# A Mamba tower on one core: convolution at unit 14, tokens at units 26 to 29, two early decays, rstd in PSUM, a hinted loop

## Chip, cores and metric

One core of one Trainium2 chip. The time is that of one execution on the device in microseconds (us); lower is better.

## What is computed

32 images of 256 x 256 x 4 become 257 tokens of 256 channels each. Layer 0 runs four Mamba blocks on every image, two forward and two backward, and merges them; a mixture of experts follows, then attention and a feed-forward part that keeps half of the tokens. The change touches the Mamba blocks alone:

```python
def _mamba_block(x, in_w, conv_w, conv_b, A_log, xd_w, xB_w, xC_w, dtp_w, dtp_b, D, out_w, g, b):
    xn = _layer_norm(x, g, b)
    xs, z = jnp.split(xn @ in_w, 2, axis=-1)
    xc = silu(causal depthwise conv of xs, 4 taps, + conv_b)
    delta = jax.nn.softplus(xc @ xd_w @ dtp_w + dtp_b)
    Bm, Cm = xc @ xB_w, xc @ xC_w
    dA = jnp.exp(delta[..., None] * -jnp.exp(A_log))
    dBx = (delta * xc)[..., None] * Bm[:, :, None, :]
    y = _ssm_scan(dA, dBx, Cm) + D * xc          # h = dA * h + dBx; y = sum_n h * C
    return y * jax.nn.silu(z) @ out_w + x
```

512 inner channels (4 groups of 128) with 16 states each; all in float32.

## The kernel before

`mamba_phase` writes out the queue of every engine by hand. The images go in 16 groups of two; a group has four **jobs**, one for each block (0, 2, 1, 3 in this order). A job has 64 scans, one for each of 4 channel groups and 16 states, over both images at once (128 partitions x 512 tokens). Two scans make a **unit**: 32 units a job. Job 0 of the first group and the last three jobs are unrolled; in between a loop of 15 iterations runs jobs 1, 2, 3 and 4, where job 4 is the first job of the next group (`run`). Each engine has its own loop, without a barrier.

For state s the work goes through the engines like this:

- ScalarE: `decays` writes exp(delta x a) to one of `NDP` = 2 PSUM banks (`decay`), two states ahead of the scan.
- GpSimd: `b_times_u` writes b x u to one of four buffers (`bu`); for every fourth state, s % 4 == 1 (`POOL_C`), it also multiplies h by c.
- VectorE: `scan`, and `c_times_h` for the other three of four states. So an even unit has two scans and one product, an odd one two and two.
- TensorE: `add_state` transposes ch into `y_ps` and adds it up (4 transposes a state). After 16 states ScalarE copies the sum (`token_rows`), TensorE turns it back (`channel_rows`), and VectorE multiplies it by the gate (`output`): y0 to y2 within the job, y3 in unit 1 of the next.

Beside the scans of job jj the engines prepare job jj + 1, at the units that the functions `after_even` and `after_odd` of ScalarE and the `period`s of TensorE and VectorE name: the gates and their Silu (units 5 to 9), centring and variance (from `norm_at`), the inverse deviation as exp(-0.5 ln(var + eps)), the input product, the convolution from `CONV_AT` = 15, its Silu at unit 24, projections (`xp`), the four step inputs (`dt0` to `dt3`) and the softplus of the step size. A Silu needs another table in ScalarE than Exp and Ln do, so two table loads stand around it. In job 2 the tokens of the next group are built as well (`tokens`, 64 matmuls on TensorE in four quarters, then two copies on ScalarE), from eight pieces of x that SP brings into two buffers (`load_x`).

All these products go to three PSUM banks, `w_ps`, which are handed round by a list of keys (`preparation`, `one_job`, `later_keys`): key i may write its first bank when key i - 2 has been read, and its second when key i - 1 has:

```python
def banks(name, g, jj):
    odd = slot(name, g, jj) % 2
    if bank_count(name) == 1:
        return w_ps[:, 2 * odd, :]
    return w_ps[:, 2:0:-1, :] if odd else w_ps[:, 0:2, :]
```

When the projections are there, SP stores b and c and reads them back, broadcast to all partitions, in eight pairs of 514 KB transfers (`bring_bc`). The rest of the program, `tail_phase`, is the same before and after.

## Time and profile before

| | |
|---|---|
| median of 3 runs | 10373.58 us (10369.56 to 10376.43) |
| profiled execution | 10389.18 us; its span 10387.4 us |
| busy: TensorE, VectorE, ScalarE, GpSimd | 8344 us (80%), 8088 (78%), 5899 (57%), 7060 (68%) |
| mean granted clock of TensorE | 0.87 |
| the Mamba stage (144 to 8662 us) | 8518 us, 64 jobs |

The profile names an instruction by its line, engine, operation and the tiles it writes and reads; PE is TensorE, PEld its weight loads, DVE VectorE, ACT ScalarE, POOL GpSimd. A "wait" is idle time of an engine and what ended it. A granted clock of 1.00 is 2.4 GHz, 0.50 is 1.2 GHz. An fp32 matmul shows as two instructions, a transpose as one. The shares of the whole span mix the Mamba stage with the tail, so they say little of either.

### The profile page before, as it was taken

What the parts mean: (1) busy time and instruction counts of PE and PEld (TensorE: products, weight loads), DVE (VectorE), ACT (ScalarE), POOL (GpSimd) and SP (SyncE); (2) the same over time, 40 slices, a digit from 0 to 9 for tenths busy, and PEclk for the clock granted to TensorE, in tenths of its full rate; (3) what the DMA queues carried; (4) which work ended last, traced back from release to release, by engine and by line L of the source; (5) the groups of instructions that cost most, each with busy time, mean ns of one, the idle gap of its engine ahead of it and who ended that gap; (6) DMA issues with size and microseconds to landing.
All of it is one profiled execution on the core that took longest, in us unless ns stands there. A gap on an engine that the chain in (4) does not pass through costs nothing. (4 is left out here: it accounts for less than half of the span.)

```text
span 10387.4 us, 152898 instructions
## 1 busy us (share of the span) xinstructions
PE 8344.1 (80%) x42776; PEld 6881.5 (66%) x42776; DVE 8087.7 (78%) x10482; ACT 5899.2 (57%) x9202; POOL 7059.5 (68%) x7227
## 2 busy tenths in 40 slices
PE   5877777777878787878787877787877776999998
PEld 4666666666666666666666666676666664777776
DVE  4888889888988888888898888888888894333332
...
GB/s 93 94 89 99 92 98 91 99 92 93 92 94 93 90 98 93 90 79 90 89 98 93 98 91 97 93 98 92 90 93 96 92 90 25 11 10 10 12 9 9
DMA packets 414916, 819.68 MB, mean 79 GB/s; under 512 B 148919, under 2 KB 194139, under 8 KB 414043
## 3 DMA queue, kind: packets, MB, share of 16 engines
...
## 5 line engine op out<-in xcount | busy, mean ns | idle before, releaser
L776 ACT ACTIVATE decay<-delta,neg_a 128x512 f32<-128x512 f32 x4096 | 2793.0, 688 | 2484.5 <-DVE h_ps L978 1112.7
L544 POOL TENSOR_TENSOR bu<-b_all,u_buf 128x512 f32<-128x512 f32 x3072 | 3579.4, 1191 | 151.6 <-DVE h_ps L978 148.3
L978 DVE TENSOR_TENSOR_SCAN h_ps<-decay,bu 128x512 f32<-128x512 f32 x2304 | 2782.6, 1222 | 454.6 <-ACT decay L776 376.3
L1233 PE MATMUL y_ps<-ident,ch 128*128 128x128 f32 x16384 | 2579.9, 309 | 637.4 <-DVE ch L998 362.7
L1233 PEld LDWEIGHTS y_ps<-ident,ch 128*128 128x128 f32 x16384 | 2226.7, 161 | 1016.2 <-DVE ch L998 484.4
L556 POOL TENSOR_TENSOR ch<-ch,c_all 128x512 f32<-128x512 f32 x1024 | 1325.5, 1294 | 1112.1 <-DVE ch L978 910.0
L998 DVE TENSOR_TENSOR ch<-h_ps,c_all 128x512 f32<-128x512 f32 x3072 | 1977.2, 671 | 0.0
L547 POOL TENSOR_TENSOR bu<-b_all,u_buf 128x514 f32<-128x514 f32 x1024 | 1245.6, 1237 | 66.8 <-issue 56.3
L1117 PE MATMUL w_ps<-xn,in_w 128*128 128x257 f32 x4096 | 1074.8, 408 | 170.5 <-ACT xn L665 83.6
L982 DVE TENSOR_TENSOR_SCAN h_ps<-decay,bu 128x256 f32<-128x256 f32 x1536 | 1046.7, 737 | 125.3 <-POOL bu L547 98.2
L1117 PEld LDWEIGHTS w_ps<-xn,in_w 128*128 128x128 f32 x4096 | 799.9, 206 | 320.2 <-issue 81.1
L1576 POOL TENSOR_TENSOR rstd_F<-h_F 128x514 f32<-128x514 f32 x16 | 17.5, 1095 | 1429.1 <-DMA h_F<-h_mid 1429.1
L978 DVE TENSOR_TENSOR_SCAN ch<-decay,bu 128x512 f32<-128x512 f32 x768 | 926.2, 1206 | 55.4 <-ACT decay L776 54.0
L1117 PE MATMUL w_ps<-xs_pad,diag_store 128*128 128x257 f32 x4096 | 950.9, 380 | 0.0
L1117 PEld LDWEIGHTS w_ps<-xs_pad,diag_store 128*128 128x128 f32 x4096 | 746.5, 190 | 91.3
L1117 PE MATMUL w_ps<-dtbc,dt_w 32*128 32x257 f32 x1024 | 443.4, 551 | 247.9 <-ACT dtbc L707 127.6
L1117 PE MATMUL w_ps<-sz,out_w 128*128 128x257 f32 x2048 | 507.4, 391 | 119.1 <-ACT x_b L762 59.1
L1117 PEld LDWEIGHTS w_ps<-sz,out_w 128*128 128x128 f32 x2048 | 379.6, 193 | 182.8 <-ACT x_b L762 66.5
L1226 PE MATMUL y_ps<-skip_diag,xc 128*128 128x128 f32 x2048 | 347.4, 324 | 172.6 <-ACT y_t L751 172.5
L1117 PEld LDWEIGHTS w_ps<-dtbc,dt_w 32*128 32x128 f32 x1024 | 216.2, 246 | 391.6 <-ACT rstd L718 184.7
L1226 PEld LDWEIGHTS y_ps<-skip_diag,xc 128*128 128x128 f32 x2048 | 317.1, 232 | 215.8 <-ACT y_t L751 211.0
L1245 PE MATMUL w_ps<-ident,y_t 128*128 128x128 f32 x1024 | 187.5, 314 | 259.1 <-ACT y_t L751 259.1
(258 smaller groups left out, 11583.9 us busy)
## 6 DMA issues: line engine op xcount, KB each, us to landing
b_all<-bc_dram SPq DMA_DIRECT2D x512, 514.0 KB, 8.6
c_all<-bc_dram SPq DMA_DIRECT2D x512, 514.0 KB, 10.0
...
diag_store<-diag_dram SPq DMA_DIRECT2D x256, 256.0 KB, 2.9
x_in<-in_x SPq DMA_DIRECT2D x128, 256.0 KB, 2.6
...
skip_diag<-skip_dram SPq DMA_DIRECT2D x64, 256.0 KB, 4.1
...
```

The lines of the kernel that those rows point to most:

```text
L544: pool.tensor_tensor(bu[:, s % NBU, 0:NB * L].rearrange("p (b t) -> p b t", b=NB), b_all[:, n // NU, n % NU, :, 1:], u_buf[:, c % 2, :, 1: ...
L547: pool.tensor_tensor(bu[:, s % NBU, :], b_all[:, n // NU, n % NU, :, :].rearrange("p b s -> p (b s)"), u_buf[:, c % 2, :, :].rearrange("p ...
L556: pool.tensor_tensor(h, h, c_all[:, n // NU, n % NU, :, 1:], ALU.mult).then_inc(pool_c_done, 1)
L776: func(decay[:, s % NDP, :].rearrange("p (b t) -> p b t", b=NB), delta[:, c, :, 1:S], ACT.Exp, scale=neg_a[:, k, c, n:n + 1]).then_inc(dec ...
L978: dve.tensor_tensor_scan(h, decay[:, s % NDP, :], bu[:, s % NBU, 0:NB * L], 0.0, ALU.mult, ALU.add).then_inc(scan_done, 1)
L982: last = dve.tensor_tensor_scan(h[:, cols], decay[:, s % NDP, cols], bu[:, s % NBU, b * S + 1:(b + 1) * S], bu[:, s % NBU, b * S:b * S + 1 ...
L998: dve.tensor_tensor(ch[:, s % NPR, :].rearrange("p (b t) -> p b t", b=NB), h_ps[:, h_slot(s), :].rearrange("p (b t) -> p b t", b=NB), c_al ...
L1117: last = pe.matmul(w[0:rows, b, 0:S], lhs, rhs, start=(i == 0), stop=(i == len(terms(b)) - 1))
L1226: pe.matmul(y_ps[:, k, :], xc[:, jj % 2, c, b, 1 + half * P:1 + (half + 1) * P], skip_diag[:, jj % 2, c, :], start=(k == 0), stop=False, s ...
L1233: last = pe.matmul(y_ps[:, k, :], ch[:, s % NPR, k * P:(k + 1) * P], ident[:, :], is_transpose=True, start=False, stop=(n == NST - 1 and k ...
L1245: last = pe.matmul(w[:, k * P:(k + 1) * P], y_t[:, k, :], ident[:, :], is_transpose=True, start=True, stop=True, skip_group_check=True)
L1576: pool.tensor_tensor(rstd[s][:, :, :], h[s][:, 0, :, :], h[s][:, 1, :, :], ALU.add).then_inc(h_summed[s], 1)
```

## The change

- The convolution starts at unit 14, and all that follows it comes a unit earlier: the Silu at unit 23, projections at 24, step inputs at 25, 26, 30 and 31. y2 is turned at unit 26 instead of 25; y1 stays at 18, where the convolution's second half used to begin behind it and now comes ahead.
- Decays 50 and 51 (`EARLY`) go to two banks of `w_ps` that idle between the convolution and the projections, right ahead of the Silu (`early_decays`). The copy of the rows of y2 comes behind the Silu.
- The tokens' products move from units 10 to 13 of job 2 to units 26 to 29, their two copies on ScalarE to 28 and 30. SP asks for the first two pieces of x at the start of job 2 and for the others between the pairs of `bring_bc`.
- The inverse deviation stays in its PSUM banks; the products with it stand inside unit 13, and the gain and bias half a unit earlier. After a job 4 the normalization starts at unit 10, not 11.
- The loop carries a hint for the branch back.

```diff
@@ -25,7 +25,8 @@
...
 BLOCK_OF_JOB = (0, 2, 1, 3)
-CONV_AT = 15
+CONV_AT = 14
+EARLY = 2 * (CONV_AT + 9) + 4, 2 * (CONV_AT + 9) + 5
 EPS = 1e-5
@@ -49,8 +50,7 @@
...
-        first = norm[:2] + ["t0"] + norm[2:] + ["t1"] if tokens else norm
-        steps = first + conv + ["xp", "dt0", "dt1", "dt2", "dt3"]
+        steps = norm + conv + ["early", "xp", "dt0", "dt1"] + (["t0", "t1"] if tokens else []) + ["dt2", "dt3"]
         return [(name, 4 if name in ("t0", "t1") else jj) for name in steps]
@@ -66,10 +66,8 @@
...
-        for name, before in [("y2", "xp"), ("y1", "cv1")] + [("y0", "t1"), ("y0", "xs0")]:
+        for name, before in [("y2", "dt1"), ("y1", "xs2"), ("y0", "xs0")]:
             at = [i for i, key in enumerate(keys) if key[0] == before]
-            if name == "y0" and ((name, jj) in keys or before == "t1" and not at):
-                continue
             keys = keys[:at[0]] + [(name, jj)] + keys[at[0]:] if at else [(name, jj)] + keys
@@ -102,14 +100,14 @@
...
     def y_at(jj):
-        return (14 if jj == 4 else 12), CONV_AT + 3, CONV_AT + 10
+        return (14 if jj == 4 else 12), 18, 26
...
     def norm_at(jj):
-        return 11 if jj == 4 else 9
+        return 10 if jj == 4 else 9
@@ -246,7 +244,7 @@
...
         rstd_ready = sem("rstd_ready")
-        xhat_ready = sem("xhat_ready")
+        rstd_logs = sem("rstd_logs")
         xn_ready = sem("xn_ready")
@@ -314,7 +312,7 @@
...
             period(0, 0, True, False)
-            with eng.Fori(0, GROUPS - 1) as g:
+            with nc.Fori(0, GROUPS - 1, engines=[eng.engine], hint_back_edge=True) as g:
                 for jj in (1, 2, 3, 4):
@@ -388,10 +386,12 @@
...
-            def load_x(g, jj):
-                for n in range(8):
+                    if jj == 3 and not is_final(g) and n in (1, 2, 3):
+                        load_x(g, 4, (2 * n, 2 * n + 1))
+            def load_x(g, jj, part=range(8)):
+                for n in part:
                     c, b, half = n // 4, n // 2 % 2, n % 2
@@ -433,6 +433,8 @@
...
+                if jj == 2 and not is_final(g):
+                    load_x(g, 4, range(2))
                 if not first:
@@ -443,8 +445,6 @@
...
                     load_weights(jj + 1)
-                    if jj == 2 and not is_final(g):
-                        load_x(g, 4)
                     load_skip(g, jj + 1)
@@ -653,6 +653,12 @@
...
                 w = banks(name, g, jj)
+                if kind == "job":
+                    func(w[:, :, 0:S], w[:, :, 0:S], ACT.Ln, bias=eps_t[:, 0:1]).then_inc(rstd_logs, 1)
+                    act.wait_ge(rstd_logs, job_count(g, jj, 1, 1))
+                    func(w[:, :, 0:S], w[:, :, 0:S], ACT.Exp, scale=-0.5).then_inc(rstd_ready, 1)
+                    return
                 func(rstd[:, :, :], w[:, :, 0:S], ACT.Ln, bias=eps_t[:, 0:1]).then_inc(read_of(name, g, jj), 1)
@@ -660,7 +666,7 @@
...
                 k = BLOCK_OF_JOB[jj % 4]
-                act.wait_ge(xhat_ready, job_count(g, jj, 1, 1))
+                act.wait_ge(read_of("var", g, jj), nth("var", g, jj))
                 for c in range(CM):
@@ -761,7 +767,19 @@
...
-            def decays(g, jj, s):
+            def early_decays(g, jj):
+                k = BLOCK_OF_JOB[jj % 4]
+                w = banks("early", g, jj + 1)
+                for c in (2, 3):
+                    act.wait_ge(read_of(f"cv{c}", g, jj + 1), nth(f"cv{c}", g, jj + 1))
+                for i, s in enumerate(EARLY):
+                    c, n = s // NST, s % NST
+                    func(w[:, i, :].rearrange("p (b t) -> p b t", b=NB), delta[:, c, :, 1:S], ACT.Exp,
+                         scale=neg_a[:, k, c, n:n + 1]).then_inc(decays_ready, 1)
+                act.sem_inc(full_of("early", g, jj + 1), 1)
+            def decays(g, jj, s, behind=0):
@@ -771,8 +789,8 @@
...
-                if positive(job_count(g, jj, STATES, s + 1 - NDP)):
-                    act.wait_ge(scan_done, job_count(g, jj, STATES, s + 1 - NDP))
+                if positive(job_count(g, jj, STATES, s + 1 - NDP - behind)):
+                    act.wait_ge(scan_done, job_count(g, jj, STATES, s + 1 - NDP - behind))
                 func(decay[:, s % NDP, :].rearrange("p (b t) -> p b t", b=NB), delta[:, c, :, 1:S], ACT.Exp,
@@ -817,6 +835,9 @@
...
                     conv_output(g, jj, c + 1)
+                act.wait_ge(read_of("cv3", g, jj), nth("cv3", g, jj))
+                act.sem_inc(full_of("early", g, jj), 1)
+                act.sem_inc(read_of("early", g, jj), 1)
                 conv_silu(g, jj)
@@ -846,11 +867,11 @@
...
                     centred(g, jj + 1, 1)
-                if jj == 2 and not is_final(g) and u == 12:
-                    tokens(g, 4, 0)
+                if jj == 2 and not is_final(g) and u in (28, 30):
+                    tokens(g, 4, (u - 28) // 2)
                 if u == norm_at(jj) + 3:
                     inverse_deviation("job", g, jj + 1)
-                if u == norm_at(jj) + (4 if jj == 4 else 5):
+                if jj == 4 and u == norm_at(jj) + 4:
                     gain_and_bias(g, jj + 1)
@@ -885,8 +906,8 @@
...
                     centred(g, jj + 1, 0)
-                if jj == 2 and not is_final(g) and u == 14:
-                    tokens(g, 4, 1)
+                if jj != 4 and u == norm_at(jj) + 4:
+                    gain_and_bias(g, jj + 1)
                 if u == CONV_AT + 1:
@@ -902,18 +923,21 @@
...
+                if not last and s in EARLY:
+                    return
                 if not (last and s >= STATES):
-                    decays(g, jj, s)
+                    decays(g, jj, s, behind=NDP if not last and s - NDP in EARLY else 0)
...
                     lead(g, jj, NU * u + NDP, last)
-                    if u % PAIRS == 1 and u // PAIRS != 3 and not (first and u == 1):
+                    if u % PAIRS == 1 and not (first and u == 1):
                         token_rows(g, jj - (u == 1), (u // PAIRS - 1) % CI)
...
                     lead(g, jj, NU * u + NDP + 1, last)
-                    if u == silu_at(jj)[1]:
-                        token_rows(g, jj, u // PAIRS - 1)
+                    if NU * u + 2 * NDP in EARLY and not last:
+                        early_decays(g, jj)
                     after_odd(g, jj, u, first, last)
@@ -940,9 +964,10 @@
...
                 dst = x_f if kind == "tok" else cen
+                inverse = rstd[:, :, :] if kind == "tok" else banks("var", g, jj)[:, :, 0:S]
                 for c in range(CM):
-                    last = dve.tensor_tensor(dst[:, c, :, :], cen[:, c, :, :], rstd[:, :, :], ALU.mult)
-                last.then_inc(x0_ready if kind == "tok" else xhat_ready, 1)
+                    last = dve.tensor_tensor(dst[:, c, :, :], cen[:, c, :, :], inverse, ALU.mult)
+                last.then_inc(x0_ready if kind == "tok" else read_of("var", g, jj), 1)
@@ -961,7 +986,18 @@
...
-            def scan(g, jj, s, b):
+            def decay_of(g, jj, s, last):
+                if s in EARLY and not last:
+                    return banks("early", g, jj + 1)[:, EARLY.index(s), :]
+                return decay[:, s % NDP, :]
+            def early_read(g, jj):
+                dve.wait_ge(scan_done, job_count(g, jj, STATES, EARLY[-1] + 1))
+                dve.sem_inc(read_of("early", g, jj + 1), 1)
+            def scan(g, jj, s, b, last):
                 inside = s not in POOL_C
@@ -975,7 +1011,7 @@
...
-                    dve.tensor_tensor_scan(h, decay[:, s % NDP, :], bu[:, s % NBU, 0:NB * L], 0.0, ALU.mult, ALU.add
+                    dve.tensor_tensor_scan(h, decay_of(g, jj, s, last), bu[:, s % NBU, 0:NB * L], 0.0, ALU.mult, ALU.add
                                            ).then_inc(scan_done, 1)
@@ -1053,23 +1089,27 @@
...
                     for b in range(NB if s < NST else 1):
-                        scan(g, jj, s, b)
+                        scan(g, jj, s, b, last)
                     if u - 1 in y_at(jj):
                         output(g, jj, y_at(jj).index(u - 1))
+                    if jj != 4 and not last and u == norm_at(jj) + 4:
+                        normalize("job", g, jj + 1)
                     if jj == 4 and u in (6, 8):
...
                         step_size(*size, 0)
-                    scan(g, jj, s + 1, 0)
+                    scan(g, jj, s + 1, 0, last)
                     if s + 1 in POOL_C and s < NST:
                         c_times_h(g, jj, s)
-                        scan(g, jj, s + 1, 1)
+                        scan(g, jj, s + 1, 1, last)
                     else:
                         if s < NST:
-                            scan(g, jj, s + 1, 1)
+                            scan(g, jj, s + 1, 1, last)
                         c_times_h(g, jj, s)
...
                             c_times_h(g, jj, s + 1)
+                    if s in EARLY and not last:
+                        early_read(g, jj)
                     if size:
@@ -1084,7 +1124,7 @@
...
                         normalize("tok", g, 4)
-                    if u == norm_at(jj) + (3 if jj == 4 else 4):
+                    if jj == 4 and u == norm_at(jj) + 3:
                         normalize("job", g, jj + 1)
@@ -1298,8 +1338,6 @@
...
                         centre(g, jj + 1, [u - norm_at(jj)])
-                    if jj == 2 and not is_final(g) and 10 <= u < 14:
-                        tokens(g, 4, (u - 10) // 2, (u - 10) % 2)
                     if u == norm_at(jj) + 2:
@@ -1321,6 +1359,8 @@
...
                         step_input(g, jj + 1, steps.index(u))
+                    if jj == 2 and not is_final(g) and 26 <= u < 30:
+                        tokens(g, 4, (u - 26) // 2, (u - 26) % 2)
```

**Place 1**, ScalarE around the Silu of the convolution in job 1. L692 (now L698) copies the convolution's last output, L751 (L757) the rows of y2, L698 and L699 (L704, L705) load the tables. Before:

```order
L692 ACTIVATE xc<-w_ps,conv_b 128x514
L775 REGISTER_ALU
L776 ACTIVATE decay<-delta,neg_a 128x512
L751 ACTIVATE y_t<-y_ps 128x512
L698 ACT_TABLE_LOAD
L698 ACTIVATE xc<-xc 128x2056
L699 ACT_TABLE_LOAD
L775 REGISTER_ALU
L776 ACTIVATE decay<-delta,neg_a 128x512
L775 REGISTER_ALU
L776 ACTIVATE decay<-delta,neg_a 128x512
```

Now:

```order
L698 ACTIVATE xc<-w_ps,conv_b 128x514
L793 REGISTER_ALU
L794 ACTIVATE decay<-delta,neg_a 128x512
L778 ACTIVATE w_ps<-delta,neg_a 128x512 x2
L704 ACT_TABLE_LOAD
L704 ACTIVATE xc<-xc 128x2056
L705 ACT_TABLE_LOAD
L793 REGISTER_ALU
L794 ACTIVATE decay<-delta,neg_a 128x512
L757 ACTIVATE y_t<-y_ps 128x512
L793 REGISTER_ALU
L794 ACTIVATE decay<-delta,neg_a 128x512
```

The two decays to `w_ps` are new ahead of the first table load, the copy of y_t has gone behind the second.

**Place 2**, TensorE behind the same Silu, in job 2. `xc,xp_w` are the projections, `dtbc,dt_w` a step input, `ident,y_t` turns y2, `skip_diag` starts the sum of the last 16 states. Before:

```order
L1221 REGISTER_ALU
L1226 MATMUL y_ps<-skip_diag,xc 128x128 x4
L1231 REGISTER_ALU
L1233 MATMUL y_ps<-ident,ch 128x128 x4
L1229 REGISTER_ALU
L1233 MATMUL y_ps<-ident,ch 128x128 x4
L1245 MATMUL w_ps<-ident,y_t 128x128 x4
L1117 MATMUL w_ps<-xc,xp_w 64x257 x8
L1231 REGISTER_ALU
L1233 MATMUL y_ps<-ident,ch 128x128 x4
L1231 REGISTER_ALU
L1233 MATMUL y_ps<-ident,ch 128x128 x4
```

Now:

```order
L1266 MATMUL y_ps<-skip_diag,xc 128x128 x4
L1271 REGISTER_ALU
L1273 MATMUL y_ps<-ident,ch 128x128 x4
L1269 REGISTER_ALU
L1273 MATMUL y_ps<-ident,ch 128x128 x4
L1153 REGISTER_ALU
L1157 MATMUL w_ps<-dtbc,dt_w 128x257 x2
L1271 REGISTER_ALU
L1273 MATMUL y_ps<-ident,ch 128x128 x4
L1271 REGISTER_ALU
L1273 MATMUL y_ps<-ident,ch 128x128 x4
L1285 MATMUL w_ps<-ident,y_t 128x128 x4
```

y2 stood ahead of the projections and now stands behind them, four states and the first step input.

**Place 3**, TensorE and the tokens (`tok_ident,x_in`, a quarter each) in job 2. Before, at units 12 and 13:

```order
L1139 ISA
L1165 REGISTER_ALU
L1117 MATMUL w_ps<-sq,mean_w 128x257 x4
L1231 REGISTER_ALU
L1233 MATMUL y_ps<-ident,ch 128x128 x4
L1231 REGISTER_ALU
L1233 MATMUL y_ps<-ident,ch 128x128 x4
L1245 MATMUL w_ps<-ident,y_t 128x128 x4
L1129 REGISTER_ALU
L1103 REGISTER_ALU
L1134 MATMUL w_ps<-tok_ident,x_in 128x128 x8
L1231 REGISTER_ALU
```

Now, at units 26 to 28:

```order
L1285 MATMUL w_ps<-ident,y_t 128x128 x4
L1157 MATMUL w_ps<-dtbc,dt_w 128x257 x2
L1169 ISA
L1143 REGISTER_ALU
L1174 MATMUL w_ps<-tok_ident,x_in 128x128 x8
L1271 REGISTER_ALU
L1273 MATMUL y_ps<-ident,ch 128x128 x4
L1269 REGISTER_ALU
L1273 MATMUL y_ps<-ident,ch 128x128 x4
L1169 REGISTER_ALU
L1174 MATMUL w_ps<-tok_ident,x_in 128x128 x8
L1179 ISA
```

The quarters stood between y0 and the variance and now follow the second step input.

## Rows read from the trace of the kernel before

**Rows 1.** Windows: start:end, us; busy of PE, PEld, DVE, ACT, POOL; clock, DMA, GB/s.
```profile
144.00:8662.00 8518.00, 6705.30 (x35260) 5612.55 (x35260) 7555.48 (x9297) 5135.84 (x7970) 7011.83 (x7164) 0.86 0.26 92
2537.00:2673.60 136.60, 113.99 (x594) 97.60 (x593) 116.81 (x146) 80.37 (x126) 109.35 (x113) 0.87 0.29 99
2945.10:3072.80 127.70, 98.95 (x530) 81.93 (x531) 116.32 (x145) 79.03 (x123) 108.33 (x112) 0.86 0.24 81
```

**Rows 2.** Waits of VectorE: us in total, times, longest.
```profile
DVE h_ps L978 <- ACT decay L776: 376.3, 251, 3.4
...
DVE diag_store L953 <- ACT sp_l L730: 75.7, 64, 39.2
```

**Rows 3.** Timeline, VectorE, a job 3 from unit 23: start, us, instruction, idle before.
```profile
2766.51 1.22 DVE L978 TENSOR_TENSOR_SCAN h_ps<-decay,bu 128x512 f32<-128x512 f32 x1
...
2767.98 1.23 DVE L978 TENSOR_TENSOR_SCAN h_ps<-decay,bu 128x512 f32<-128x512 f32 x1 [0.24 <-POOL bu L544]
...
2780.74 1.23 DVE L978 TENSOR_TENSOR_SCAN h_ps<-decay,bu 128x512 f32<-128x512 f32 x1 [3.35 <-ACT decay L776]
...
2784.61 2.33 DVE L978 TENSOR_TENSOR_SCAN h_ps<-decay,bu 128x512 f32<-128x512 f32 x2
...
2788.04 1.22 DVE L978 TENSOR_TENSOR_SCAN h_ps<-decay,bu 128x512 f32<-128x512 f32 x1
```

**Rows 4.** Timeline, ScalarE, the same stretch.
```profile
2775.40 1.28 ACT L698 ACT_TABLE_LOAD   x1
...
2776.70 1.93 ACT L698 ACTIVATE xc<-xc 128x2056 f32<-128x2056 f32 x1
...
2779.93 1.30 ACT L776 ACTIVATE decay<-delta,neg_a 128x512 f32<-128x512 f32 x2
```

**Rows 5.** Timeline, TensorE, the same stretch.
```profile
2776.43 1.04 PE L1233 MATMUL y_ps<-ident,ch 128*128 128x128 f32 x8
...
2777.30 0.60 PE L1245 MATMUL w_ps<-ident,y_t 128*128 128x128 f32 x4
...
2778.67 3.68 PE L1117 MATMUL w_ps<-xc,xp_w 128*64 128x257 f32 x16 [0.77 <-ACT xc L698]
...
2785.40 1.13 PE L1117 MATMUL w_ps<-dtbc,dt_w 32*128 32x257 f32 x4 [2.02 <-ACT dtbc L707]
...
2788.91 1.22 PE L1117 MATMUL w_ps<-dtbc,dt_w 32*128 32x257 f32 x2 [0.73 <-ACT rstd L718]
```

**Rows 6.** A window of the same job; the 0.50 is the granted clock.
```profile
2788.60:2795.30 6.70, 6.26 (x25) 5.21 (x26) 6.70 (x8) 6.20 (x11) 6.29 (x7) 0.50 0.99 301
```

**Rows 7.** Timeline: y1 in a job 3, its TensorE, and y1 in a job 2.
```profile
2753.66 0.69 DVE L1018 TENSOR_TENSOR sz<-w_ps,sz 128x512 f32<-128x512 f32 x1 [0.84 <-PE w_ps L1245]
...
2753.46 3.63 PE L1117 MATMUL w_ps<-xs_pad,diag_store 128*128 128x257 f32 x16
...
3158.16 0.69 DVE L1018 TENSOR_TENSOR sz<-w_ps,sz 128x512 f32<-128x512 f32 x1 [1.57 <-PE w_ps L1245]
```

**Rows 8.** Groups of VectorE: busy us, mean ns, idle before.
```profile
L944 DVE TENSOR_TENSOR cen<-cen,rstd 128x514 f32<-128x514 f32 x128 | 119.9, 975 | 36.4 <-ACT rstd L659 36.4
...
L933 DVE TENSOR_TENSOR cen<-h_next,w_ps 128x514 f32<-128x514 f32 x32 | 20.6, 688 | 56.9 <-PE w_ps L1117 56.9
```

**Rows 9.** Timeline: y0 in a job 2, and a quarter of the tokens.
```profile
3134.17 0.69 DVE L1018 TENSOR_TENSOR sz<-w_ps,sz 128x512 f32<-128x512 f32 x1 [7.65 <-PE w_ps L1245]
...
3126.30 4.08 PE L1134 MATMUL w_ps<-tok_ident,x_in 128*128 128x128 f32 x16
```

**Rows 10.** DMA issues: count, KB each, median us to landing.
```profile
c_all<-bc_dram SPq DMA_DIRECT2D x512, 514.0 KB, 10.0
...
x_in<-in_x SPq DMA_DIRECT2D x128, 256.0 KB, 2.6
```

**Rows 11.** Timeline: the back edge, VectorE and GpSimd.
```profile
2945.07 1.40 DVE L982 TENSOR_TENSOR_SCAN h_ps<-decay,bu 128x256 f32<-128x256 f32 x2 [5.03 <-POOL bu L547]
...
2942.41 1.27 POOL L547 TENSOR_TENSOR bu<-b_all,u_buf 128x514 f32<-128x514 f32 x1 [4.17 <-issue]
```

## Prediction

> **What bounds the kernel now.** I read the windows first. Over the stage that the change touches, which I cut out as one window of 8518 us, VectorE is busy 7555 us (89%), GpSimd 82%, TensorE 79% and ScalarE 60% [rows 1]. VectorE's order is fixed by hand, so the stage lasts as long as its work plus its waits; the other engines matter where it waits for them. A job (one block of one pair of images) is 32 units of two states: the window of a job 1 is 127.7 us with 116.3 us of VectorE work, that of a job 2 is 136.6 us with nearly the same work [rows 1]. Then the table of waits says whose fault the rest is: 376 us for decays from ScalarE and 76 us for the logarithm of the step size are the two of this stage that I need [rows 2]. The timelines of single jobs tell where in a job they lie. The reader should see there that the same waits come at the same unit of every job.
>
> **Part 1: the convolution a unit earlier, two decays ahead, y2 a unit later.** Between the starts of units 23 and 28 VectorE takes 2788.04 - 2766.51 = 21.5 us, 3.35 of them one wait for decay 52 [rows 3], since ScalarE loads a table (1.28), runs the Silu (1.93) and loads the old table back, as long again [rows 4] while only two decays lie ready. In the change the same work follows decay 49 and the two decays of the idle banks. Counted from the start of unit 23: state 47's scan is done at 2.6 (it starts at 1.47 [rows 3] and takes 1.2); decay 49 and two early ones at 0.65 each (two took 1.30 [rows 4]) end at 4.6; table and Silu end at 7.85, the second table and decay 52 at 9.8. VectorE without this wait reaches unit 26 at 2780.74 - 2766.51 - 3.35 = 10.9, so the stall goes entirely.
>
> What is late next is y2. After the Silu TensorE has the projections (3.6), the skip products (1.0, as many as the transposes of two states), two states (0.9), the first step input (1.1), two more states (0.9) and the transposes (0.6), by the rows of each [rows 5]: 7.85 + 8.1 = 15.9. VectorE is ready for y2 at 10.9 + 2.85 + 1.14 = 14.9 (the odd unit 27 takes 3.43, its two scans 1.14 each [rows 3]; an even one has a product less, 0.59). It waits 1.0, and after y2 (0.7, and 0.4 until the next scan starts), a scan and two products it is at unit 28 at 19.2, 2.3 us sooner than now.
>
> TensorE's clock comes on top. Now a convolution runs right up to the Silu; in the change it ends two units sooner, and some 6 us with 16 short transposes lie ahead of the projections. After such stretches the granted clock was 0.50 (1.2 GHz) in this kernel: in the window at 2788.6 two products of a step input took 1.22 us, where four had taken 1.13 before it [rows 5, 6]. Work on the path then costs up to double; a stretch of 6.7 us at half clock costs 3.4 us at most. I take 1.3 us a job (most jobs pay nothing or 1.7; not all fall into it), with bounds of 0 and 3.4. Net 1.0 us, times 63 jobs with a next job: **-63 us**. By the Trainium skill (TensorE: Matmul & The Clock Gate, Part 1) an array that has idled runs at 1.2 GHz and comes back to 2.4 only once it has been kept busy; it would put every job's projections at the half clock, and the sum by it is rival 2. The row of 0.50 agrees that such stretches occur; whether this one becomes one no run here shows.
>
> **Part 2: y1.** The unit of y1 stays 18, but the 16 products of convolution 1 now stand ahead of it. From the start of unit 17: copy of the rows at 2.5 (scan 1.2, decay 0.7, copy 0.6), skip 1.0, two states 0.9, convolution 3.5 [rows 7], two states 0.9, transposes 0.6: 9.4. VectorE wants it at 3.4 + 2.85 + 1.14 = 7.4, so it waits 2.0 instead of 0.84 [rows 7]. A job 2 waits 1.57 there already [rows 7], and I take jobs 4 to be like it, so I charge the 1.1 us to the 31 jobs 1 and 3: **+34 us** (bounds 0 and 63 x 1.5 = 95).
>
> **Part 3: the logarithm.** Everything behind the Silu comes a unit earlier, so the 0.58 us before the step size goes ((75.7 - 39.2) / 63 [rows 2]; the 39.2 is the first job's): **-36 us**. It could not give more, and costs nothing while TensorE is less than a unit late.
>
> **Part 4: inverse deviation in PSUM.** Two products a job now read rstd from PSUM. Read from SBUF they took 0.98 us each, and the same shape with a PSUM input 0.69 [rows 8]: 2 x 0.29 x 63 = **-37 us**. For the job after a job 4 the chain now starts in the very unit of the gate's Silu; I cost that at nothing: ScalarE's two centring copies come behind its Silu and eat what the earlier start brings.
>
> **Part 5: the tokens.** Now they sit at units 10 to 13 of job 2 and hold y0 back by 7.65 us [rows 9]. A job 2 is 8.9 us longer than a job 1 [rows 1]; less the 0.7 of y1, 8.2 us can go per group. In units 26 to 29 they hang on ScalarE instead: its copy of t0 stands ahead of decay 59. From the end of y2's transposes: step input 0.9, a quarter of the tokens 3.8 [rows 9], two states 0.9, the next quarter 3.8, and 1.3 for pieces of x that are asked for only when one is used up (2.6 us to land [rows 10]): 10.8. ScalarE then needs 2.7 for copy, powers and decay; VectorE comes for decay 59 at 7.4. So it waits 6.1 us, and 2.1 are left: 15 x 2.1 = **-31 us**, with bounds of -123 (no wait at all) and the loss of rival 3.
>
> **Part 6: the loop's back edge.** VectorE stands still for 5.03 us between the last instruction of job 4 and the first of job 1, waiting for GpSimd, whose own 4.17 us are put down to nothing but issue [rows 11]. Each engine's sequencer branches there for itself, so all of them stand still together. Nothing in this trace has a hinted branch; the bounds are 0 and all of it, 14 x 5.0. I take all of it, as GpSimd begins to stand still at 2942.41 - 4.17 = 2938.2 and VectorE only at 2945.07 - 5.03 = 2940.0 [rows 11]: without the branch GpSimd would have its first product of job 1 (1.27) ready in time: **-70 us**. The Trainium skill (Runtime: NRT & Kernel Launch, Instruction fetch mechanics) says that a taken branch to code not in the instruction memory waits for a DMA, and Advanced Engine Details and Errata (Control Flow Timing) gives some 108 ns for a compare-and-branch; by these the estimate would be 14 x 4.9 = 69 us.
>
> **Sum.** -63 + 34 - 36 - 37 - 31 - 70 = -203 us on a span of 10387.4. The profiled execution took 10389.2, 15.6 more than the median of the runs; from the median 10373.6 the sum gives 10170. What 0.2% (21 us) can't tell from no change, I count as the same.
>
> **Rivals.**
> 1. *The hint does nothing.* The stall at the first unit of job 1 stays at 5 us: 10240. Against it speaks only that the wait is pure issue. 0.12.
> 2. *TensorE is at half clock behind every Silu.* y2 waits 1.0 + 3.4 us: 63 x (3.4 - 1.3) = 132 more, 10302. For it: the granted clock falls wherever the work is thin [rows 6]. 0.13.
> 3. *The tokens starve ScalarE, and the kernel gets slower.* Between pieces of x SP now issues the 514 KB broadcasts of b and c, of which the latter takes 10.0 us to land where a piece takes 2.6 [rows 10]. If a piece queues behind them and lands after 10.0, each of the three turns costs 7.4: 6.1 + 22.2 = 28.3 us of waiting against 8.2 removed. That is +302 in the place of -31: 10373.6 - 172 + 302 = 10504. It decides from a landing of 7.6 us on (15 x (6.1 + 3 x 5.0 - 8.2) = 194 us). Against it: the broadcasts of a job come one pair per unit, and three pieces are asked for by then. 0.07.
> 4. *TensorE stays at full clock.* 63 x 1.3 = 82 less: 10088. 0.17.
> The forecast itself, within some 50 us of 10170, has 0.48, and 0.03 is left for mishaps of no one name.
>
> **How the numbers follow.** The likeliest case gives 10170. The range reaches down past case 4 with some of the tokens' bound (10050) and up to case 1 with half of case 2 (10290); rival 3 and the rest lie outside. Faster takes all but rival 3 and some of the rest: 0.88; same 0.04; slower 0.08.
>
> **What would show it.** The wait for a decay at unit 26 gone; a wait of 1 to 3 us at y2 in unit 27 (long with a granted clock of 0.50 there, short without); y1's wait at 2 us; the product with rstd at 0.69; unit 13 of job 2 as short as in job 1, and a wait of 6 us for decay 59 in it; the first scan of job 1 straight behind job 4. The prediction is wrong if GpSimd, with 82% now, becomes what VectorE waits for, if the tokens' wait is over 20 us, or if the projections start later than the Silu's end.

## The result, and the profile after

| | before | after |
|---|---|---|
| median of 4 runs each | 10375.01 us (10369.56 to 10381.79) | 10297.75 us (10291.67 to 10303.34) |
| ratio | | 0.9925, 95% interval 0.9908 to 0.9942 |
| profiled execution | 10389.18 us | 10301.12 us, span 10299.2 |
| end of the Mamba stage | 8662 us | 8569 us |

So the change is 77 us faster, where 203 were forecast, and the time lies just above the range (10290). The direction was right, and the size was not. (The two profiled executions differ by 88 us and their stages by 93, since the one before was 14 us above its median and the one after only 3.)

The windows of the changed kernel: the stage from 144 us to its end, then a job 1 and a job 2.

```profile
144.00:8569.30 8425.30, 6705.40 (x35260) 5524.77 (x35260) 7525.31 (x9298) 5134.66 (x7970) 6977.26 (x7164) 0.87 0.27 93
2906.97:3034.01 127.04, 99.98 (x530) 81.56 (x529) 116.44 (x146) 79.34 (x124) 108.92 (x113) 0.86 0.27 92
3034.01:3170.19 136.18, 111.80 (x589) 94.34 (x588) 115.88 (x145) 78.76 (x124) 109.53 (x113) 0.89 0.30 99
```

Against [rows 1] VectorE's work fell by 30 us and the stage by 93. A job 1 and a job 2 take what they took before, to 0.7 us. To see where the time went I cut every job of the loop at the first scan of some units, and took the difference of each stretch, mean of 15 iterations (us, after less before):

| units | 0-9 | 9-12 | 12-16 | 16-20 | 20-22 | 22-28 | 28-32 | job |
|---|---|---|---|---|---|---|---|---|
| job 1 | -0.1 | 0.0 | -1.7 | +1.3 | -0.3 | 0.0 | 0.0 | -0.8 |
| job 2 | 0.0 | 0.0 | -7.9 | -0.2 | -0.3 | +0.6 | +7.9 | +0.1 |
| job 3 | -0.5 | 0.0 | -0.8 | +1.1 | -0.3 | -1.1 | +0.1 | -1.5 |
| job 4 | -0.6 | -0.1 | -0.3 | +1.4 | -0.3 | +0.1 | -4.5 | -4.3 |
| all four | -1.2 | -0.1 | -10.7 | +3.6 | -1.1 | -0.4 | +3.5 | -6.5 |

-6.5 us by 15 iterations are -97. One column stands out by what it does not show: units 22 to 28, where the Silu is, give next to nothing (-0.4 for all four jobs). The tokens' 7.9 only change their place. The 4.5 at the end of job 4 are the back edge of the loop. Now the rows.

VectorE's waits in the stage. The wait for decays has grown from [rows 2], and that for the turned rows (`sz`) is large:

```profile
DVE h_ps L1014 <- ACT decay L794: 402.8, 178, 7.7
DVE sz L1054 <- PE w_ps L1285: 293.8, 214, 2.3
```

VectorE behind the Silu in a job 1, units 26 and 27 (start, duration, instruction, idle before it):

```profile
3007.26 1.20 DVE L1014 TENSOR_TENSOR_SCAN ch<-decay,bu 128x512 f32<-128x512 f32 x1
3008.37 0.67 DVE L1034 TENSOR_TENSOR ch<-h_ps,c_all 128x512 f32<-128x512 f32 x1
3010.68 1.23 DVE L1014 TENSOR_TENSOR_SCAN h_ps<-decay,bu 128x512 f32<-128x512 f32 x1 [1.64 <-ACT decay L794]
3013.79 0.69 DVE L1054 TENSOR_TENSOR sz<-w_ps,sz 128x512 f32<-128x512 f32 x1 [1.88 <-PE w_ps L1285]
3014.86 1.23 DVE L1014 TENSOR_TENSOR_SCAN h_ps<-decay,bu 128x512 f32<-128x512 f32 x1 [0.38 <-POOL bu L544]
```

The stall of 3.35 at unit 26 [rows 3] is gone, and three waits stand a unit later, 3.9 us together. ScalarE and TensorE of the same stretch, both cut to the chain:

```profile
3002.04 1.92 ACT L704 ACTIVATE xc<-xc 128x2056 f32<-128x2056 f32 x1
3003.97 1.28 ACT L705 ACT_TABLE_LOAD   x1
...
3009.39 0.59 ACT L713 ACTIVATE dtbc<-w_ps 64x514 f32<-64x514 f32 x1 [2.33 <-PE w_ps L1157]
3009.88 1.29 ACT L794 ACTIVATE decay<-delta,neg_a 128x512 f32<-128x512 f32 x2
```

```profile
3004.01 5.26 PE L1157 MATMUL w_ps<-xc,xp_w 128*64 128x257 f32 x16 [3.34 <-ACT xc L704]
3009.20 1.16 PE L1266 MATMUL y_ps<-skip_diag,xc 128*128 128x128 f32 x8
3010.20 1.04 PE L1273 MATMUL y_ps<-ident,ch 128*128 128x128 f32 x8
3011.16 1.13 PE L1157 MATMUL w_ps<-dtbc,dt_w 32*128 32x257 f32 x4
3012.22 1.09 PE L1273 MATMUL y_ps<-ident,ch 128*128 128x128 f32 x8
3013.15 0.60 PE L1285 MATMUL w_ps<-ident,y_t 128*128 128x128 f32 x4
```

TensorE stands idle 3.34 us for the Silu, then takes 5.26 us for the projections. ScalarE's copy of them (L713) stands in its queue ahead of decay 54, so VectorE waits for decay 54 until 3010.6. The turn of y2 comes behind 3.9 us of other work. The windows of the idle time, the first half of the projections and the time behind it (the third number from the end is the granted clock):

```profile
3001.00:3004.00 3.00, 0.00 (x0) 0.00 (x0) 3.00 (x5) 2.97 (x3) 3.00 (x3) 0.97 0.00 0
3004.00:3007.20 3.20, 3.19 (x8) 1.80 (x9) 3.20 (x4) 3.04 (x4) 3.20 (x4) 0.50 0.00 0
3007.30:3010.00 2.70, 2.70 (x16) 1.76 (x15) 1.74 (x3) 0.61 (x2) 2.31 (x7) 1.00 0.00 0
```

The group of all projections, the changed kernel and then, in a fence of its own, the kernel before (busy us, mean ns of one, idle time ahead):

```profile
L1157 PE MATMUL w_ps<-xc,xp_w 128*64 128x257 f32 x1008 | 343.1, 515 | 212.8 <-ACT xc L704 212.8
```

```profile
L1117 PE MATMUL w_ps<-xc,xp_w 128*64 128x257 f32 x1008 | 232.0, 382 | 48.4 <-ACT xc L698 48.4
```

Job by job it is plainer still: before, TensorE idled 0.77 us ahead of the projections and they took 3.68 us in 63 of 64 jobs; after, it idles 3.3 to 3.4 us and they take over 4 us in 55 of 64 jobs (median 5.36, up to 6.62). The 60 jobs of the changed kernel's loop sort themselves by it (us, mean in brackets):

| projections took | jobs | VectorE's wait for decay 54 | its wait for y2 | units 22 to 28 |
|---|---|---|---|---|
| 3.68 | 9, all of them jobs 3 | none | 1.69 | 22.3 to 22.4 |
| 5.22 to 5.37 | 33 | 1.25 to 1.75 (1.54) | 1.88 | 23.9 to 24.4 (24.25) |
| 6.40 to 6.61 | 18, 12 of them jobs 2 | 2.43 to 2.72 (2.55) | 1.88 | 25.1 to 25.5 (25.20) |

Before, units 22 to 28 took 24.35 us in every job. So a job at full clock gains 2.0 us there, most jobs gain 0.1, and the longest projections lose 0.85. The whole difference passes through the wait for decay 54; the wait for y2 hardly moves. In the nine jobs of the first row TensorE had stood idle just as long (3.3 us) as in the others.

The groups of VectorE that changed (rstd read from PSUM, to be held against [rows 8]; the step size's first instruction), and the back edge, where VectorE's first scan of job 1 now starts without a wait (L983 is the last work of job 4):

```profile
L978 DVE SCALAR_TENSOR_TENSOR diag_store<-diag_store 128x514 f32<-128x514 f32 x127 | 121.7, 958 | 0.0
...
L969 DVE TENSOR_TENSOR cen<-cen,w_ps 128x514 f32<-128x514 f32 x126 | 81.2, 687 | 13.9 <-DVE sz L1054 10.8 <-ACT w_ps L660 3.0
```

```profile
2906.17 0.88 DVE L983 SCALAR_TENSOR_TENSOR cen<-cen,sq 128x514 f32<-128x514 f32 x1
2906.97 1.39 DVE L1018 TENSOR_TENSOR_SCAN h_ps<-decay,bu 128x256 f32<-128x256 f32 x2
```

The tokens in a job 2: VectorE in unit 29, ScalarE's copy with the decay behind it, and TensorE's quarters:

```profile
3156.71 1.23 DVE L1014 TENSOR_TENSOR_SCAN h_ps<-decay,bu 128x512 f32<-128x512 f32 x1 [6.97 <-ACT decay L794]
```

```profile
3154.05 0.69 ACT L623 ACTIVATE h_next<-w_ps,tok_wb 128x512 f32<-128x512 f32 x1 [6.41 <-PEq L1180]
...
3155.92 0.67 ACT L794 ACTIVATE decay<-delta,neg_a 128x512 f32<-128x512 f32 x1
```

```profile
3143.27 4.00 PE L1174 MATMUL w_ps<-tok_ident,x_in 128*128 128x128 f32 x16
...
3149.82 4.10 PE L1174 MATMUL w_ps<-tok_ident,x_in 128*128 128x128 f32 x16 [1.67 <-DMA x_in<-in_x]
```

### The profile page after: what moved, and what is told of

The parts are those of the page before. It is cut to its first block and busy times, and to the rows that moved or that the text cites. A ratio compares the mean times of both kernels' runs of the same rounds, so it can differ in the third digit from the quotient of the medians.

```text
span 10299.2 us, 152957 instructions
## 1 busy us (share of the span) xinstructions
PE 8347.5 (81%) x42776; PEld 6796.5 (66%) x42776; DVE 8057.0 (78%) x10482; ACT 5898.0 (57%) x9202; POOL 7025.0 (68%) x7227
## 5 line engine op out<-in xcount | busy, mean ns | idle before, releaser
L794 ACT ACTIVATE decay<-delta,neg_a 128x512 f32<-128x512 f32 x3970 | 2712.6, 688 | 2269.8 <-DVE h_ps L1014 1062.9
L1014 DVE TENSOR_TENSOR_SCAN h_ps<-decay,bu 128x512 f32<-128x512 f32 x2178 | 2629.7, 1222 | 503.9 <-ACT decay L794 402.8
L1273 PE MATMUL y_ps<-ident,ch 128*128 128x128 f32 x16384 | 2488.7, 300 | 552.9 <-DVE ch L1034 434.6
L1273 PEld LDWEIGHTS y_ps<-ident,ch 128*128 128x128 f32 x16384 | 2111.7, 155 | 926.9 <-DVE ch L1034 578.5
L1157 PE MATMUL w_ps<-xn,in_w 128*128 128x257 f32 x4096 | 1104.4, 415 | 157.8 <-ACT xn L671 63.9
L1157 PE MATMUL w_ps<-xc,xp_w 128*64 128x257 f32 x1024 | 348.5, 515 | 217.0 <-ACT xc L704 217.0
L1157 PE MATMUL w_ps<-dtbc,dt_w 32*128 32x257 f32 x1024 | 398.2, 510 | 77.8 <-ACT rstd L724 75.3
L1157 PEld LDWEIGHTS w_ps<-xc,xp_w 128*64 128x64 f32 x1024 | 185.0, 187 | 366.6 <-issue 213.0
```

The costliest lines, as they stand in the source:

```text
L794: func(decay[:, s % NDP, :].rearrange("p (b t) -> p b t", b=NB), delta[:, c, :, 1:S], ACT.Exp, scale=neg_a[:, k, c, n:n + 1]).then_inc(dec ...
L1014: dve.tensor_tensor_scan(h, decay_of(g, jj, s, last), bu[:, s % NBU, 0:NB * L], 0.0, ALU.mult, ALU.add).then_inc(scan_done, 1)
L1157: last = pe.matmul(w[0:rows, b, 0:S], lhs, rhs, start=(i == 0), stop=(i == len(terms(b)) - 1))
L1273: last = pe.matmul(y_ps[:, k, :], ch[:, s % NPR, k * P:(k + 1) * P], ident[:, :], is_transpose=True, start=False, stop=(n == NST - 1 and k ...
```

## The experiments

Each was timed beside the kernel before, in five rounds. The groups of runs had their own kernel before (medians 10384, 10375 and 10383 us), so the times are compared by their ratios; a ratio is known to about 0.0013, 14 us, and the difference of two gains a little worse than that. "Gain" below is one less the ratio, times 10375, in us; the changed kernel has 78 by that.

| run | median us | ratio, 95% interval | gain |
|---|---|---|---|
| e1_hint_alone | 10301.42 | 0.9923, 0.9909 to 0.9936 | 80 |
| e2_hint_and_rstd | 10322.97 | 0.9947, 0.9934 to 0.9961 | 55 |
| e9_norm_at_10 | 10316.78 | 0.9934, 0.9920 to 0.9948 | 68 |
| e3_tokens_at_10 | 10351.10 | 0.9971, 0.9959 to 0.9983 | 30 |
| the change | 10297.75 | 0.9925, 0.9908 to 0.9942 | 78 |
| e10_rstd_in_sbuf | 10331.40 | 0.9950, 0.9937 to 0.9964 | 52 |
| e4_y2_first | 10209.98 | 0.9832, 0.9819 to 0.9846 | 174 |
| e5_warm | 10209.86 | 0.9838, 0.9824 to 0.9851 | 168 |
| e6_y1_first | 10230.99 | 0.9859, 0.9844 to 0.9874 | 146 |
| e11_y1_and_copy | 10243.43 | 0.9868, 0.9853 to 0.9883 | 137 |
| e7_both_and_softplus | 10216.38 | 0.9844, 0.9830 to 0.9857 | 162 |
| e8_both_and_warm | 10104.35 | 0.9740, 0.9726 to 0.9753 | 270 |
| e12_all_and_copy | 10051.02 | 0.9679, 0.9666 to 0.9692 | 333 |

**From the kernel before to the change, one part at a time.** First the hint alone, on the kernel before.

```diff
-            with eng.Fori(0, GROUPS - 1) as g:
+            with nc.Fori(0, GROUPS - 1, engines=[eng.engine], hint_back_edge=True) as g:
```

> The kernel before with the hinted loop and nothing else. My theory: the 5.0 us that VectorE stands still at the first unit of job 1 go, 14 to 15 times, and nothing else moves: 70 to 75 us less, about 10302. That would be nearly all that the whole change gave (77 us), so the other five parts together would give nothing. Rival: the stall only went because the changed order around it left GpSimd ahead; then the hint alone gives under 35 us and the first wait of job 1 stays above 2 us.

It gave 80, all that the whole change gives. The forecast of part 6 was 70; the waits inside the jobs stay nearly as they were (1.5 us less over four jobs). So the other parts come to nothing together.

Added to it, the inverse deviation in PSUM, its two uses at their old places.

```diff
+                if kind == "job":
+                    func(w[:, :, 0:S], w[:, :, 0:S], ACT.Ln, bias=eps_t[:, 0:1]).then_inc(rstd_logs, 1)
+                    act.wait_ge(rstd_logs, job_count(g, jj, 1, 1))
+                    func(w[:, :, 0:S], w[:, :, 0:S], ACT.Exp, scale=-0.5).then_inc(rstd_ready, 1)
+                    return
...
+                inverse = rstd[:, :, :] if kind == "tok" else banks("var", g, jj)[:, :, 0:S]
```

> The kernel before with the hint and the inverse deviation left in PSUM, its products with it at their old place. My theory: two products a job at 0.69 us in the place of 0.98 give 37 us more than the hint, about 10265, which is faster than the changed kernel. Rival: GpSimd, whose share is 82%, or the bank that is now held until VectorE has read it (for y0 and the first input product) gives it back: within 10 us of the hint alone.

25 us slower than e1, not 37 faster. The first theory fell, and the rival was right in its second half: jobs 1, 3 and 4 got shorter by 0.5, 1.3 and 1.6 us, but a job 2 longer by 4.7, in a new wait of 4.85 us for a decay at unit 16. TensorE there:

```profile
3102.86 0.60 PE L1252 MATMUL w_ps<-ident,y_t 128*128 128x128 f32 x4
3108.33 4.00 PE L1141 MATMUL w_ps<-tok_ident,x_in 128*128 128x128 f32 x16 [4.86 <-DVE cen L951]
```

The second half of the tokens may write its first bank only when the variance's banks have been read. That used to be done by ScalarE's logarithm; now it is done by VectorE's product, which stands behind the late y0. And ScalarE's copy of those tokens stands ahead of a decay. A part that is worth 37 us by its own instruction costs 25 where another part is missing.

Next the convolution with everything that hangs on it. The changed kernel with only the tokens put back differs from e2 in just that (convolution and Silu a unit earlier, early decays, y1 and y2, and the normalization of job 4).

```diff
-                    if jj == 2 and not is_final(g) and 26 <= u < 30:
-                        tokens(g, 4, (u - 26) // 2, (u - 26) % 2)
...
+                    if jj == 2 and not is_final(g) and 10 <= u < 14:
+                        tokens(g, 4, (u - 10) // 2, (u - 10) % 2)
```

> The changed kernel with the tokens' products, their copies, their keys and SP's loads of x back at units 10 to 14 of job 2. My theory: in the changed kernel the tokens cost 8.7 us of waiting for decays at units 29 and 31 of job 2 and about 0.7 at unit 27, in the old place 7.7 before y0: so the same within 1 us a group, 10283 to 10313. Rival, my prediction's part 5: the old place is 2.1 us a group dearer, 31 us more, 10329.

Parts 1, 2 and 3 and job 4 together: from e2 (55) to e3 (30), 25 us lost, where the forecast had 63 + 36 - 34 = 65 gained. And the tokens' move, from e3 (30) to the change (78), gains 48, more than the 31 of part 5 and against my theory of 0: beside PSUM rstd the old place has e2's wait too. The two parts go together. (By the job table the move is worth nothing, -7.9 and +7.9 us; no run has it beside an rstd in SBUF against the same kernel without it.)

From e2 to e3 a job 4 went from 132.7 to 135.7 us (medians). Is it the normalization at unit 10? This run is e2 with that alone:

```diff
     def norm_at(jj):
-        return 11 if jj == 4 else 9
+        return 10 if jj == 4 else 9
```

> e2_hint_and_rstd (10323) with one number changed: the normalization after a job 4 starts at unit 10 in the place of 11, as in the changed kernel; the convolution stays at 15. It asks why a job 4 takes 135.7 us in the changed kernel and 132.7 in e2. Theory 1: the earlier centring, whose two copies on ScalarE now stand right behind the gate's Silu and ahead of decays 27 and 29, costs it: job 4 at 135 to 136, 15 x 3 = 45 more, about 10365. Theory 2: the convolution at 14 costs it: job 4 stays at 132.7 and the time is the same within 10 us.

A job 4 takes 133.0 us: theory 2. Its waits for decays at unit 13 do double (2.3 to 4.6 us), but of the 1.9 us that it waited at unit 14 for rstd and a decay 0.9 are left (now at unit 13), and y1's wait falls from 2.0 to 0.8: together they pay for it. With the convolution at 14 as well (e3) y1 waits 2.3 again, and 1.4 us for decays at units 17 and 18 come on top.

The other side of the pair: the changed kernel with part 4 taken back.

```diff
-                inverse = rstd[:, :, :] if kind == "tok" else banks("var", g, jj)[:, :, 0:S]
+                inverse = rstd[:, :, :]
```

> The changed kernel with the inverse deviation back in SBUF. In e2 against e1 PSUM cost 22 us, though each of the two products got 0.29 us shorter, since a job 2 got 4.4 us longer: its second half of the tokens stood behind the banks of the variance, and the copy of it ahead of a decay. Theory: in the changed kernel the tokens stand elsewhere, so PSUM gives what the products say, and without it the time is 37 us higher, 10325 to 10340. Rival: the products' gain is eaten by GpSimd or by the held banks here too, and it is the same within 10 us.

26 us by the ratios, 34 by the medians: theory, within the noise. Part 4 is worth most of its 37 where the tokens are out of its way. Not all of the difference is its own, though: without it the projections ran over 4 us in 63 of 64 jobs in the place of 55, and 0.8 of the 2.7 us by which the four jobs got longer lie in units 22 to 28.

**What stands behind the Silu.** Seven products ahead of the projections, in the idle time, into the bank that they will overwrite:

```diff
+            def warm(g, jj):
+                w = banks("xp", g, jj)
+                bank_free("xp", g, jj, 0)
+                for i in range(7):
+                    pe.matmul(w[0:RNK + 2 * NST, 0, 0:S], xp_w[:, i % CI, :], xc[:, (jj + 1) % 2, i % CI, 0, :], start=True, stop=True)
...
                     if step == 10:
+                        warm(g, jj + 1)
                         projections(g, jj + 1)
```

> The changed kernel with seven extra products of TensorE ahead of every projection, while it would stand idle for the Silu (3.35 us). They write nothing that is kept. My theory: the projections take 5.4 us in 55 of 64 jobs, since the granted clock is 0.50 behind that idle time, and 3.7 us otherwise; with work in the gap all take 3.7, the two waits of unit 27 lose the 1.6 us together, 52 jobs, and the time falls by 60 to 100 us, to about 10215. Rival: the clock is not what they wait for (the length comes from reading xc beside GpSimd, say); then the projections stay at 5.4 or start later behind the extra products, and the time is the same or up to 30 us more.

90 us faster than the change, by adding work. The rows of TensorE in a job 1 (the seven, then the projections), and VectorE's, where the scan of unit 27 starts without a wait and y2 is still late:

```profile
2978.51 3.25 PE L1233 MATMUL w_ps<-xc,xp_w 128*64 128x257 f32 x14
2981.92 3.68 PE L1157 MATMUL w_ps<-xc,xp_w 128*64 128x257 f32 x16 [0.16 <-ACT xc L704]
```

```profile
2987.01 1.23 DVE L1014 TENSOR_TENSOR_SCAN h_ps<-decay,bu 128x512 f32<-128x512 f32 x1
2990.12 0.69 DVE L1054 TENSOR_TENSOR sz<-w_ps,sz 128x512 f32<-128x512 f32 x1 [1.88 <-PE w_ps L1291]
```

The projections take 3.68 us in every job of the loop, the wait for decay 54 is gone in all of them, and units 22 to 28 are 7.1 us shorter over four jobs. The rival (the length comes from something else than the clock) is refuted. Together with the table by length of the projections this shows what ate part 1: the half clock, by way of decay 54. The wait for y2 stays, at 1.69 to 1.88 us.

Then the order: y2 turned straight behind the projections, and ScalarE's copy of the projections behind decay 55.

```diff
-        for name, before in [("y2", "dt1"), ("y1", "xs2"), ("y0", "xs0")]:
+        for name, before in [("y2", "dt0"), ("y1", "xs2"), ("y0", "xs0")]:
...
-                if u == CONV_AT + 11:
+                if u == CONV_AT + 12:
                     projections(g, jj + 1)
...
                         projections(g, jj + 1)
+                        channel_rows(g, jj, 2)
```

> The changed kernel with two orders changed: TensorE turns y2 straight behind the projections, ahead of the skip products, states 48 and 49 and the first step input; and ScalarE copies the projections' rows behind decay 55, half a unit later, in the place of ahead of decay 54. VectorE's order is the same. My theory: the Silu's stall was not removed but moved to unit 27, where VectorE waits 1.65 us for decay 54 (it stands behind the copy, which waits for projections that take 5.4 us at the half clock in the place of 3.7) and then 1.9 for y2 (behind 4.5 us of TensorE's other work). Both and the 0.4 behind them go: 3.5 us a job, 63 jobs, 220 less, about 10080. Rival: GpSimd, which caught up in these waits, becomes what VectorE waits for at units 27 to 31, and half or less of it comes out: above 10190.

96 us faster than the change, under half of what I expected. Both waits of unit 27 are gone, and this is what came:

```profile
2997.71 1.23 DVE L1014 TENSOR_TENSOR_SCAN h_ps<-decay,bu 128x512 f32<-128x512 f32 x1 [1.24 <-ACT decay L794]
2999.51 1.22 DVE L1014 TENSOR_TENSOR_SCAN ch<-decay,bu 128x512 f32<-128x512 f32 x1 [0.57 <-ACT decay L794]
```

Not GpSimd, as the rival had it, but the next copy on ScalarE that stands ahead of a decay: the softplus, which waits for the first step input, which waits for the copy that I had put later. The projections are as slow as before (over 4 us in 52 of 64 jobs). In a job 2 the tokens' wait grew from 6.97 to 8.9 us.

**y1.** TensorE turns it in unit 17, ahead of convolution 1.

```diff
-        for name, before in [("y2", "dt1"), ("y1", "xs2"), ("y0", "xs0")]:
+        for name, before in [("y2", "dt1"), ("y1", "cv1"), ("y0", "xs0")]:
...
-                    if u in y_at(jj):
+                    if u in (y_at(jj)[0], 17, y_at(jj)[2]):
```

> The changed kernel with one order changed: TensorE turns y1 in unit 17, ahead of the 16 products of convolution 1, in the place of behind them and behind states 34 and 35. Theory: VectorE's wait of 1.9 to 2.2 us at unit 19 goes, with the bubble of 0.4 behind it; 63 jobs by 2.0 to 2.4 us: 125 to 150 less, about 10160. Rival: convolution 1 ends 0.6 us later and the Silu with it, or GpSimd is what VectorE finds next; then under 60 less.

68 us, near the rival's 60 and half of the theory. The wait for y1 went, and decay 39 took its place, behind ScalarE's copy (L698) of the convolution that now ends 0.6 us later. ScalarE and VectorE in a job 1:

```profile
2972.24 0.69 ACT L698 ACTIVATE xc<-w_ps,conv_b 128x514 f32<-128x514 f32 x1 [3.70 <-PE w_ps L1157]
2972.83 0.68 ACT L794 ACTIVATE decay<-delta,neg_a 128x512 f32<-128x512 f32 x1
```

```profile
2973.63 1.23 DVE L1014 TENSOR_TENSOR_SCAN h_ps<-decay,bu 128x512 f32<-128x512 f32 x1 [2.15 <-ACT decay L794]
```

That copy half a unit later:

```diff
-                if u in (CONV_AT + 3, CONV_AT + 4):
-                    conv_output(g, jj + 1, u - CONV_AT - 3)
+                if u == CONV_AT + 3:
+                    conv_output(g, jj + 1, 0)
...
+                if u == CONV_AT + 4:
+                    conv_output(g, jj + 1, 1)
```

> e6_y1_first (10231) with ScalarE's copy of convolution 1 half a unit later, behind decay 39 in the place of ahead of it. In e6 the wait for y1 (2.0 us at unit 19) was replaced by one of 1.95 for decay 39, which stood behind that copy. Theory: this wait goes too, 63 jobs by 1.9: about 10110, if nothing is next. Rival: the next thing late (GpSimd's product at unit 19, 0.4, the second input product, whose copy then is ahead of decay 41) takes over half: above 10170.

A miss, in the rival's range: the wait of 1.95 is gone (0.4 and 0.6 are left), and the time is that of e6. Of the 5.9 us that units 16 to 20 gave over four jobs, units 20 to 22 took back 2.7 and units 22 to 28 took 4.3. TensorE now idles 4.06 us ahead of the projections instead of 3.35, and all 64 of them take over 5 us. The same step at full clock (e8 to e12 below) gives 6.2 in units 16 to 20, and units 22 to 28 take back 1.2 only; so about 3 of the 4.3 were the half clock's.

**Together.** e7 has y1 as in e6, y2 and copy as in e4, and the first softplus half a unit later; e8 is e7 with the seven products; e12 is e8 with the copy of e11.

```diff
-                if u in (CONV_AT + 13, CONV_AT + 14):
-                    softplus_powers(g, jj + 1, u - CONV_AT - 13)
+                if u == CONV_AT + 13:
+                    softplus_start(g, jj + 1, 0)
+                if u == CONV_AT + 14:
+                    softplus_powers(g, jj + 1, 1)
...
-                if u in (CONV_AT + 12, CONV_AT + 13):
-                    softplus_start(g, jj + 1, u - CONV_AT - 12)
+                if u == CONV_AT + 13:
+                    softplus_powers(g, jj + 1, 0)
+                    softplus_start(g, jj + 1, 1)
```

> The changed kernel with y1 ahead of convolution 1 (as alone in another run), y2 straight behind the projections with their copy behind decay 55 (as in e4_y2_first, 10210), and the first softplus pair of ScalarE half a unit later, behind decay 56, since in e4_y2_first VectorE waited 0.9 to 1.25 and 0.57 us at unit 28 for decays 56 and 57, which stood behind ScalarE's wait for the first step input. Theory: the gains add up, 88 for y2, 130 for y1, 80 for unit 28: about 10010. Rival: GpSimd takes over, at 85% of the stage, and the sum is under half of it: above 10150.

> e7_both_and_softplus with the seven extra products ahead of every projection. Theory: with both orders mended the length of the projections is what unit 27 and 28 wait for, and full clock gives up to 1.6 us a job, 50 to 100 less than e7. Rival: in e7 nothing waits for the projections any more, so it is the same within 15 us.

> e8_both_and_warm (10104) with the same half unit for ScalarE's copy of convolution 1. Theory: VectorE's wait of 1.9 to 2.2 us for decay 39 at unit 19 goes from all jobs, 63 x 1.9 = 120 less: about 9985. Rival: what is next takes over half: above 10045.

e7 is no better than e4 alone: the gains do not add up. That is the rival's range, but not for its reason (GpSimd): the projections take 6.15 us in the median, over 4 us in 60 of 64 jobs, and VectorE's wait for decays at unit 29 is 1.7 to 1.8 us in jobs 1, 3 and 4. e8 gains 108 more, a little above its theory. e12 gains 63 more than e8 by the ratios and 53 by the medians, about half of its theory: 10051 lies just inside the rival's range (above 10045). At **10051 us, 0.9679 of the kernel before (0.9666 to 0.9692)**, e12 beats both kernels. The largest wait left in it is that of the tokens: VectorE waits 11.5 us for a decay at unit 29 of each job 2.

## Why the prediction was wrong

- **Part 1 (Silu, -63; it gave 6).** This is the step that failed most. The stall at unit 26 went entirely, as said, and y2 is late, as said. What was wrong is the path and the price of TensorE's clock. (a) The sum let the slow projections act on y2 alone. They act by another path, which the sum did not contain: ScalarE's copy of the projections stands ahead of decay 54, and VectorE waits for that decay, 1.65 us in jobs 1 and 4, 2.33 in job 2, and 2.1 in 6 of 15 jobs 3. (b) *"I take 1.3 us a job ... not all fall into it"*: nearly all fall into it. The first half of the projections runs at a lowered clock in 55 of 64 jobs, and they take 1.7 us longer each and up to 2.9. Over four jobs this costs 7.1 us in units 22 to 28 (e5), 1.8 a job. Before, the idle time is 0.77 us and the change makes it 3.35, which I could have worked out: all of the Silu's table and work. By the Trainium skill (TensorE: Matmul & The Clock Gate, Part 1) an idle array drops to 1.2 GHz and must be kept busy to come back; the trace agrees in those 55 jobs, and e5 shows it from the other side, but in 9 jobs the same idle time left the granted clock at 1.00. (c) y2 waits 1.7 to 1.9 us and not 1.0, even at full clock (e5). Units 22 to 28 gave 0.4 us per four jobs, 6 us in all. At full clock (e5) they give 7.5, 1.9 a job, where the forecast without its 1.3 for the clock was 2.3. So of the 0.9 us a job that were missing, 0.5 are the clock's and 0.4 the rest.
- **Part 2 (y1, +34).** The wait is 2.15, 1.94, 1.91 and 2.24 us in jobs 1 to 4, for a forecast of 2.0. But units 16 to 20 cost 3.6 us per iteration, about 55 us: job 4, which I had set like job 2 and not charged, pays 1.4 as well. There y1 had waited 1.9 us already; what is new are 1.2 us of waits for decays at units 17 and 18.
- **Part 3 (logarithm, -36).** The wait of 36.5 us went from all jobs. In its place the instruction behind it got slower, 90.9 to 121.7 us in total. Net -6: *"costs nothing"* failed. The reason, read from the traces and not tested by a run, is in the last section: without the wait GpSimd still runs beside this instruction.
- **Part 4 (rstd, -37).** Right to the microsecond in its own group: 118.6 to 81.2 us. In the time it shows only with part 5 (-25 in e2; +26 in e10, in part by the clock).
- **Part 5 (tokens, -31).** y0's wait went, and the wait for decay 59 is 6.97 for 6.1. Not priced were 1.75 us for decay 63 behind the second copy. Per job 2 the move is nothing, -7.9 and +7.9. It is worth 48 us only against an old place that part 4 has made worse. The 0.7 us by which a job 2 waits longer for decay 54 than a job 1 are the clock's again: its projections took 6.4 us in 12 of 15 cases. With the tokens at unit 10 (e3) they took 5.1 to 5.4; why is open. The pieces of x land after 4.0 us, so rival 3 (7.6 and more) was rightly small. Two readings of the sum were a little off: its chain adds up to 10.7 and not 10.8, and over the 15 jobs of each kind a job 2 was 8.2 us longer than a job 1 where the single windows gave 8.9.
- **Part 6 (back edge, -70).** Right in mechanism: 80 us (e1), 14 waits of 5 us and some smaller ones. Rival 1 is refuted. That the wait had been one for code is supported by the instruction queues of the stage, whose packets fell from 339 and 504 to 315 and 453 with the hint alone; by the Trainium skill (Runtime: NRT & Kernel Launch, Instruction fetch mechanics) a taken branch to code that isn't there waits for such a fetch. No row shows the fetch itself.

The terms that missed are 57 + 21 + 30 + 31 us too hopeful, and part 6 was 10 too careful: 129, for the 126 between 203 and 77. Of the rivals, 2 came within 5 us of the time, at 0.13, and that is luck. It was right that the clock falls behind nearly every Silu. But it priced this at 3.4 us a job, 132 us over the forecast, and at y2; the clock's cost was 1.8 a job, some 31 over the forecast, and at decay 54. The rest of the way to 10298 came from y2's own wait and from parts 2, 3 and 5. The sign given for it (a long wait at y2 when the clock is 0.50, a short one when not) did not work either: that wait is 1.88 us in a job 1 with slow projections and with fast ones.

What stays open: whether the early decays alone, with the rest as before, would gain; no run has the convolution at 15 with the tokens moved. Why some projections take 6.4 and not 5.4 us, and why nine of them, behind the same idle time, took 3.68.
